# Tail of the attention in a fused decoder kernel: the last slots' work in an order written out step by step

## The reference, cut to what matters

```
x1     = x + softmax(q k^T * 1.5 / sqrt(128)) v Wout + bout       # per head, summed over 8 heads
z      = layernorm(x1);  logits = z @ router_w                    # 2048 x 8
expert = argmax(logits);  gate = 1 / sum(exp(logits - max))
pos    = running count of the tokens of that expert;  keep = pos < 256
expert_in[expert, pos] += z                                       # a scatter of rows
out    = x1 + gate * keep * (gelu(expert_in w1[e]) w2[e])[expert, pos]
```

## Time and profile before

| what | value |
| --- | --- |
| median of 3 runs | 1421.51 us (1419.95 to 1425.56) |
| the profiled execution, its own time | 1420.5 us |
| its span from first to last instruction | 1418.8 us |
| mean granted TensorE clock | 0.982 |
| PE busy over the span | 1330.4 us (94%) |
| DVE busy | 1121.2 us (79%) |
| ACT busy | 901.1 us (64%) |
| POOL busy | 881.1 us (62%) |
| last exponentials of the attention end | about 1249 us |
| first matmul of the first expert | 1314.32 us |

### The profile page before, as it was taken

The page is one execution under the profiler, slowest core; times in us unless marked ns, Lnnn a source line. Parts: engine busy times, 40 slices in busy tenths (PEclk is TensorE's granted clock), DMA queues, the critical chain, the costliest instruction groups (busy, mean ns, idle before and its releaser), DMA issues.

```text
span 1418.8 us, 20495 instructions
## 1 busy us (share of the span) xinstructions
PE 1330.4 (94%) x7244; PEld 1091.6 (77%) x7244; DVE 1121.2 (79%) x1711; ACT 901.1 (64%) x1325; POOL 881.1 (62%) x535
## 2 busy tenths in 40 slices
PE   3999999988999989999999999999999999994998
PEld 3777887887878767777777777787777778773997
DVE  6779988976811778989898998989898898985454
ACT  3534433224565577877777777777878777676674
POOL 1400011213431199998999989989989989874453
PEclk9999999999999999999999999999999999996899
DMA  9102003124666488887888888878878878787572
GB/s 278 20 9 67 2 18 109 47 76 136 232 178 213 151 229 216 212 208 192 213 210 193 216 192 208 219 179 215 210 197 210 210 175 211 182 201 263 183 243 80
DMA packets 171955, 241.22 MB, mean 170 GB/s; under 512 B 34020, under 2 KB 77414, under 8 KB 171857
## 3 DMA queue, kind: packets, MB, share of 16 engines
q1 hardware_dynamic: 156704, 210.21, 58.1%
q10 hardware_dynamic: 13104, 23.86, 5.0%
q0 software_dynamic: 2048, 5.90, 1.1%
HBM read 64.79 MB, written 41.32 MB: 75 GB/s over the span
## 4 chain that ended last, share of the span: by engine, by line
PE 51%; DVE 15%; ACT 5%; issue 4%; DMA 1%; POOL 0%; SPq 0%; ACTq 0%; DVEq 0%; POOLq 0%
PE xa_S L1476 20%; PE xa_O L1493 12%; DVE xa_mxp L1269 5%; PE xa_Y L1430 5%; PE xa_Y L1505 4%; PE ex_H L1928 3%; PE ex_Y L1940 3%; ACT xa_probs L1649 3%; PE xa_O L1430 3%; DVE xa_tq L1282 3%; DVE xa_mx_nb_rinv L1267 2%; DVE hall L1303 2%; DVE xa_mx_nb_rinv L1272 1%; DMA xa_moved<-xa_tq 0%; DVE xa_mx_nb_rinv L1298 0%
## 5 line engine op out<-in xcount | busy, mean ns | idle before, releaser
L1152 POOL TENSOR_TENSOR xa_pT<-xa_moved,xa_pT 128x1024 fp32r<-128x1024 f32 x246 | 586.1, 2406 | 35.6 <-ACT xa_pT L1643 32.4
L1476 PE MATMUL xa_S<-xa_kT,xa_qT 128*128 128x512 f32 x1536 | 397.6, 408 | 14.7 <-ACT xa_probs L1649 11.7
L1649 ACT ACTIVATE xa_probs<-xa_S,xa_mx_nb_rinv 128x1024 f32<-128x1024 f32 x256 | 286.0, 1118 | 174.6 <-DVE xa_mx_nb_rinv L1272 174.6
L1493 PE MATMUL xa_O<-xa_pT,xa_v 128*128 128x512 f32 x1536 | 375.8, 394 | 2.6 <-DVE xa_pT L1325 2.6
L1476 PEld LDWEIGHTS xa_S<-xa_kT,xa_qT 128*128 128x128 f32 x1536 | 286.3, 190 | 102.4 <-ACT xa_probs L1649 41.5
L1493 PEld LDWEIGHTS xa_O<-xa_pT,xa_v 128*128 128x128 f32 x1536 | 289.3, 189 | 68.0 <-DVE xa_pT L1325 2.9
L1282 DVE STREAM_TRANSPOSE xa_tq<-xa_probs 128x1024 f32<-128x1024 f32 x256 | 316.7, 1237 | 13.6 <-ACT xa_probs L1649 5.9
L1643 ACT ACTIVATE xa_pT<-xa_moved 128x1024 fp32r<-128x1024 f32 x254 | 253.8, 1049 | 4.1 <-DMA xa_moved<-xa_tq 3.9
L1267 DVE TENSOR_REDUCE xa_mx_nb_rinv<-xa_S 128x1 f32<-128x1024 f32 x128 | 155.6, 1215 | 79.8 <-PE xa_S L1476 77.5
L1269 DVE TENSOR_REDUCE xa_mxp<-xa_S 128x1 f32<-128x1024 f32 x128 | 157.5, 1230 | 17.7 <-PE xa_S L1476 17.7
L467 PE MATMUL fw_pp<-fw_hT,fw_wqk 128*128 128x512 f32 x384 | 100.7, 413 | 9.9 <-DVE fw_F L613 8.3
(11 more groups left out here) (228 smaller groups left out, 1812.6 us busy)
## 6 DMA issues: line engine op xcount, KB each, us to landing
xa_moved<-xa_tq SPq DMA_DIRECT2D x508, 256.0 KB, 4.5
heads_k<-ci_outs SPq DMA_DIRECT2D x32, 256.0 KB, 2.0
heads_v<-ci_outs SPq DMA_DIRECT2D x32, 256.0 KB, 2.3
heads_q<-ci_outs SPq DMA_DIRECT2D x32, 256.0 KB, 2.2
xa_chunk<-heads_v ACTq DMA_DIRECT2D x32, 256.0 KB, 3.7
ex_w1s<-in_L_ffn_w_dram SPq DMA_DIRECT2D x8, 1024.0 KB, 6.9
ex_w2s<-in_L_ffn_w_dram SPq DMA_DIRECT2D x8, 1024.0 KB, 10.0
xa_chunk<-heads_q ACTq DMA_DIRECT2D x31, 256.0 KB, 3.5
```

The costliest lines, as they stand in the source:

```text
L1152: pool.tensor_tensor(quadrants(pT[LO], r), unit_moved(r), quadrants(pT[HI], r).bitcast(F32), ALU.subtract).then_inc(lo_ready, 1)
L1476: last = pe.matmul(S[:, k], qT[a][:, i // GT % 2, q], kT[b][h % 2][:, k * 512:(k + 1) * 512], start=(n == 0), stop=(n == 2))
L1493: last = pe.matmul(O[:], v[a][:, j * P:(j + 1) * P], pT[b][:, r % PRING, k], start=(j == 0 and n == 0), stop=(j == JT - 1 and n == 2))
L1649: act.activation(probs[:, unit % RING], S[:, 2 * u:2 * u + 2].rearrange("p a b -> p (a b)"), ACT.Exp, bias=nb[:, s % 2:s % 2 + 1], scale=S ...
```

## The change

The loops over slots now end at SLOTS. What was issued behind slot 127 is written out call by call on PE, ACT and DVE. Group 31's weighted sum goes to the bank `mxp` in place of `xa_O`, and quad 2's logits and counts to S[3]. `place_rows` is split in two: the places, and the gate (`gate_rows`) with a semaphore of its own, for which the scatters wait as well. `table(0, ACT.Exp)` is dropped. Quad 3's exponentials are one activation over four tiles, of values that DVE has multiplied, with the sum taken on DVE, and two of quad 3's four tiles are scaled on DVE. DVE waits for all scatters to land before `expert_low`.

```diff
-        rp = [... for bank in (S[:, 2], S[:, 3], mxp[:], S[:, 2])]
+        rp = [... for bank in (S[:, 2], S[:, 3], S[:, 3], S[:, 2])]
...
-        END = SLOTS + 14
-        OUTPUTS = ...
-        SUMS = ...
-        ROUTING = ...
+        TAIL = SLOTS // GT - 3
+        def output_of(g):
+            return mxp if g == SLOTS // GT - 1 else O
...
             def scatter(q):
                 pool.wait_ge(slot_ready, q + 1)
+                pool.wait_ge(gated, q + 1)
                 if q < 2:
                     pool.wait_ge(scaled, q + 1)
                 else:
-                    pool.wait_ge(last_scaled, q - 1)
+                    pool.wait_ge(last_scaled, 4 if q == 2 else 6)
...
             def deviations_of_rows(q):
...
+                dve.wait_ge(rstd_rows, q + 1)
...
             def place_rows(q):
-                dve.wait_ge(expd, q + 1)
-                dve.reciprocal(rows[:, quad_rows(q), GATE], gate[:, quad(q)])
...
+            def gate_rows(q):
+                dve.wait_ge(expd, q + 1)
+                dve.reciprocal(rows[:, quad_rows(q), GATE], gate[:, quad(q)]).then_inc(gated, 1)
+            def scale_rows(tiles):
+                for i in tiles:
+                    dve.tensor_scalar(rows[:, place_of(i), 0:D], rows[:, place_of(i), X1:X1 + D], rs[:, i, 0:1],
+                                      rrstd[:, i:i + 1], ALU.subtract, ALU.mult)
...
             # VectorE behind the loop
+            transpose(SLOTS - 1, 1)
+            for k in range(2):
+                add_output(TAIL, k)
+                row_stats(TAIL, k)
+            low_parts(SLOTS - 5)
+            deviations_of_rows(0)
+            low_parts(SLOTS - 4)
+            deviations_of_rows(1)
+            choose(0)
+            low_parts(SLOTS - 3)
+            choose(1)
+            low_parts(SLOTS - 2)
+            add_outputs(TAIL + 1)
+            low_parts(SLOTS - 1)
+            statistics(TAIL + 1)
+            place_rows(0)
+            place_rows(1)
+            gate_rows(0)
+            gate_rows(1)
+            deviations_of_rows(2)
+            choose(2)
+            add_outputs(TAIL + 2)
+            place_rows(2)
+            gate_rows(2)
+            statistics(TAIL + 2)
+            choose(3)
+            deviations_of_rows(3)
+            dve.tensor_tensor(spent[:, quad(3)], ex[:, quad(3)], wide(rrstd[:, quad(3)]), ALU.mult).then_inc(rstd_rows, 1)
+            place_rows(3)
+            scale_rows(range(12, 14))
+            dve.wait_ge(expd, QUADS)
+            then(dve.reduce_sum(gate[:, quad(3)], spent[:, quad(3)], AX))
+            gate_rows(3)
+            dve.wait_ge(scattered, 16 * TILES)
             expert_low(0, w1p, w1s)
             expert_low(1, w2p, w2s)
...
             # TensorE
-                if q == 0 and g:
+                if q == 0 and 0 < g < SLOTS // GT - 1:
                     pe.wait_ge(oT_ready, g)
...
             def row_logits(q):
-                if q == QUADS - 1:
-                    pe.wait_ge(slot_ready, 1)
+                if q >= 2:
+                    pe.wait_ge(slot_ready, 2 if q == 2 else 1)
...
             # TensorE behind the loop
+            transposes_of(0)
+            weighted(SLOTS - 7)
+            out_project(TAIL, 1)
+            weighted(SLOTS - 6)
+            row_logits(0)
+            transposes_of(1)
+            weighted(SLOTS - 5)
+            row_logits(1)
+            output(TAIL + 1)
+            weighted(SLOTS - 4)
+            positions(0)
+            weighted(SLOTS - 3)
+            positions(1)
+            weighted(SLOTS - 2)
+            transposes_of(2)
+            weighted(SLOTS - 1)
+            row_logits(2)
+            output(TAIL + 2)
+            positions(2)
+            transposes_of(3)
+            row_logits(3)
+            positions(3)
...
             # ScalarE behind the loop
+            high_parts(SLOTS - 6)
+            copies(0)
+            high_parts(SLOTS - 5)
+            row_root(0)
+            row_root(1)
+            high_parts(SLOTS - 4)
+            copies(1)
+            copy_oT(TAIL + 1)
+            high_parts(SLOTS - 3)
+            row_exp(0)
+            high_parts(SLOTS - 2)
+            row_exp(1)
+            high_parts(SLOTS - 1)
+            copies(2)
+            row_root(2)
+            copy_oT(TAIL + 2)
+            scale_rows(2)
+            row_exp(2)
+            copies(3)
+            row_root(3)
+            row_exp(3)
+            scale_rows(3)
```

More of the change, by code:

```diff
@@ L847, in cross_block @@
         PJ = len(pj)
-        rp = [bank[:, 0:4 * E].rearrange("p (t e) -> p t e", e=E) for bank in (S[:, 2], S[:, 3], mxp[:], S[:, 2])]
+        rp = [bank[:, 0:4 * E].rearrange("p (t e) -> p t e", e=E) for bank in (S[:, 2], S[:, 3], S[:, 3], S[:, 2])]
         x_in = [sem(f"ci_x_in{s}") for s in range(HALVES)]
@@ L929, in among @@
             return range(EARLY + sum(AMONG[:s]), EARLY + sum(AMONG[:s + 1]))
-        END = SLOTS + 14
-        OUTPUTS = {(30, 0): 3, (30, 1): 3, (31, 0): 7, (31, 1): 7}
-        SUMS = {(30, 0): 3, (30, 1): 4, (31, 0): 7, (31, 1): 7}
-        ROUTING = {"transposes": (0, 2, 4, 8), "copies": (0, 2, 4, 8), "logits": (1, 3, 5, 9), "choose": (2, 3, 5, 9),
-                   "positions": (3, 4, 6, 10), "place": (3, 4, 6, 11),
-                   "statistics": (None, None, 4, 8), "root": (1, 1, 4, 8), "scale": (1, 2, 4, 9), "rows": (1, 2, 5, 9),
-                   "exp": (3, 3, 5, 10)}
+        TAIL = SLOTS // GT - 3
         def place_of(i):
@@ L949, in output_slot @@
         def output_slot(g, k):
-            return SLOTS + OUTPUTS[g, k] if (g, k) in OUTPUTS else (g + 1) * GT + LAG + k
+            return (g + 1) * GT + LAG + k
         def sum_slot(g, k):
-            return SLOTS + SUMS[g, k] if (g, k) in SUMS else (g + 1) * GT + LAG + 1 + k
+            return (g + 1) * GT + LAG + 1 + k
         halves_of_groups = [(g, k) for g in range(SLOTS // GT) for k in range(2)]
-        def due(what, s):
-            return [q for q, late in enumerate(ROUTING[what]) if late is not None and SLOTS + late == s]
         def finished(eng, q, k=1):
@@ L1379, in expert_low, with low_parts, add_outputs, statistics @@
                                   ALU.subtract).then_inc(e_lo, 1)
-            for s in range(END):
-                if s < SLOTS:
-                    maxima(s)
-                if 1 <= s <= SLOTS:
+            def low_parts(p):
+                low_part(2 * p)
+                low_part(2 * p + 1)
+            def add_outputs(g):
+                add_output(g, 0)
+                add_output(g, 1)
+            def statistics(g):
+                row_stats(g, 0)
+                row_stats(g, 1)
@@ L1396, in _ @@
-                for q in due("statistics", s):
-                    for k in range(2):
-                        row_stats(SLOTS // GT - 4 + q, k)
-                for q in due("scale", s):
-                    deviations_of_rows(q)
-                for q in due("choose", s):
-                    choose(q)
-                for q in due("place", s):
-                    place_rows(q)
+                transpose(s, 0)
+            transpose(SLOTS - 1, 1)
+            for k in range(2):
+                add_output(TAIL, k)
+                row_stats(TAIL, k)
@@ L1677, in row_exp @@
             def row_exp(q):
-                act.wait_ge(shifted, q + 1)
+                act.wait_ge(oh_ready, q + 1)
                 act.wait_ge(rstd_rows, q + 1)
-                for i in range(4 * q, 4 * q + 4):
-                    last = act.activation(spent[:, i], ex[:, i], ACT.Exp, scale=rrstd[:, i:i + 1], accum_out=gate[:, i:i + 1])
+                if q == QUADS - 1:
+                    act.wait_ge(rstd_rows, QUADS + 1)
+                    last = act.activation(spent[:, quad(q)], spent[:, quad(q)], ACT.Exp)
+                else:
+                    for i in range(4 * q, 4 * q + 4):
+                        last = act.activation(spent[:, i], ex[:, i], ACT.Exp, scale=rrstd[:, i:i + 1], accum_out=gate[:, i:i + 1])
                 last.then_inc(expd, 1)
@@ L1720, in _ @@
-                for q in due("copies", s):
-                    for k in range(2):
-                        copy_zt(q, k)
-                for q in due("root", s):
-                    row_root(q)
-                for q in due("rows", s):
-                    if q >= 2:
-                        table(0, ACT.Exp)
-                        scale_rows(q)
-                for q in due("exp", s):
-                    row_exp(q)
+                for c in chunks_of(s):
+                    chunk_high(c)
```

85 lines of the change are left out of this document (36 added, 49 removed).

## The result

The changed kernel took 1428.68 us (median of 7 runs, 1427.71 to 1433.02) against 1421.85 for the kernel before (7 runs, 1419.95 to 1425.56): a ratio of 1.0052, 95% interval 1.0037 to 1.0067. That is 6.8 us slower, outside the range of the prediction. The same kernel, unaltered, took 1419.54 and 1419.80 us in two later sets of runs on other occasions, while the kernel before took 1421.2 to 1421.9 in every set. The rest of this document is about that difference of 9 us.

A forecast was written before the change was run, and what follows sets the result against it. The tail was taken as bound by the order of DVE's work, then quad 3's serial chain, not transfers. Landing 4.2 us earlier less 2.6 given back is 1.6: 1421.5 - 1.6 = 1419.9 us, range 1416.5 to 1425.0.

The forecast's parts named there:

- statistics at 1291.2, choose 3 at 1293.3: DVE's tail: statistics end at 1291.2, then the choice for quad 3 follows directly and ends at 1293.3.
- low parts 127 end: DVE's tail: the last quarter's low parts end at 1277.1, 6.4 us ahead of 1283.5 in the kernel before.
- first scatter: POOL: the first scatter may start at 1281.7, 0.8 after the gate, with 1.27 from each to the next.
- last scatter: POOL: quad 3's scatters start at 1297.9, the last at 1301.7, landing at 1304.25 against 1308.47 before.
- landing to first expert: Start of the expert block: DVE's split after the landing makes this 8.45 instead of 5.85, giving 2.6 us back.
- first expert: Expert block: the first expert's matmuls begin at 1312.7, against 1314.32 in the kernel before.
- ACT's Exp load: ACT ahead of quad 3's scatters: the late table load costs 1.28, so ACT is last and rows are ready at 1297.1.
- POOL's queue becomes the bound: Rival at POOL's scatters: at pace 1.6 each, +2.3 to 1423.8, chance 0.2; at worst pace 2.3, 1434, chance 0.03.
- The table switch drains: Rival on ACT: the Exp load holds ACT another 1.4, quad 3 ready at 1298.5, kernel 1421.3; chance 0.07.
- The wait on the scatters costs nothing: Rival at the expert block: rows' transfer bounds it, not DVE's split, so all 4.2 us stay: 1417.3; chance 0.08.
- The 6.4 us go through: Rival on DVE: work behind the last low parts lies in idle time, so the kernel takes 1415.1; chance 0.04.
- The own bank: Group 31's output on PE: removes PE's wait for group 30's copy, costed at nothing because DVE is the bound there.

The follow-up runs named there:

- fourth set: The changed kernel run again, unaltered, on a later occasion beside the kernel before: 1419.54 us, ratio 0.9987; three other variants ran in the same set.
- fifth set: The changed kernel run a third time, unaltered, in a session of its own beside the kernel before: 1419.8 us, ratio 0.9986.
- The last run: The changed kernel without DVE's wait for the scatters' landing, run a second time, where nothing stalled: 1420.49 us, ratio 0.9996.
- quad 0 early: Against the changed kernel, quad 0's places and gates put right behind choose 1, so its scatters start earlier: 1420.0 us, ratio 0.999.
- the breaks on POOL: Changed kernel with a one-column POOL memset ahead of quad 1's and quad 2's scatters: 1420.0, 1419.28 and 1420.33 us in three sets.

## Why the prediction was wrong, point by point

**The step that failed** is the one sentence "statistics at 1291.2, choose 3 at 1293.3". It took for granted that quad 3's logits are known to DVE when PE has made them, as all earlier ones are. Statistics ended at 1291.6, the logits themselves at 1293.04, and choose 3 started at 1299.9. Of the 8.7 us by which it came behind the forecast, 6.8 are the late report, 1.4 the wait for matmuls that had themselves waited for a late report of the transposes, and 0.4 the statistics. The sum had no term for a late report, and the rows of the kernel before could not have priced one: its scatters come in rows of 4, with a pause at each new quad, and its logits of quad 3 are reported on time.

The same sentence puts quad 3's transposes and logits on PE at nothing, as if they always ended ahead of DVE's statistics. That fits the fourth set's run, where they end at 1291.35 and choose 3 starts right behind the statistics, and not the fifth set's, where DVE waits 1.71 us for them. It is a smaller term, left out without a reason.

**The rest of the sum held**, and the traces of the fourth and fifth set show it undisturbed:

| Step | Forecast | Result's run | Fourth set | Fifth set |
|---|---|---|---|---|
| low parts 127 end | 1277.1 | 1278.1 | 1278.5 | 1278.5 |
| first scatter | 1281.7 | 1282.6 | 1282.9 | 1283.0 |
| choose 3 starts | 1291.2 | 1299.9 | 1291.5 | 1293.0 |
| last scatter | 1301.7 | 1310.6 | 1302.4 | 1303.7 |
| landing to first expert | 8.45 | 8.0 | 8.0 | 8.0 |
| first expert | 1312.7 | 1321.1 | 1312.9 | 1314.3 |

In the landing's row the start of DVE's first split stands for the landing. The 8.0 comes out 0.45 under the forecast: 0.45 instead of 0.6 behind DVE, and 1.2 instead of 1.33 from L1961 to the matmuls make up part of it. ACT's Exp load is the last thing ahead of quad 3's scatters, as forecast: they start 0.88 behind ACT's last scaling in both undisturbed traces. The kernel's time was forecast as 1419.9 and is 1419.5 and 1419.8 where nothing stalled; the gain over the kernel before was forecast as 1.6 and is 2.3 and 1.4. That the numbers agree so closely is in part luck, as steps up to 1.4 late (low parts) and 0.45 early (the expert block) offset one another, and one program's choose 3 differs by 1.5 from trace to trace.

**The rivals.** *POOL's queue becomes the bound* named the right neighbour and the wrong victim. With DVE's wait in place the scatters never stretched: in rows of 12 and 16 all but the first took 0.97 to 1.03. What suffered was the report of another engine's work. *The table switch drains* is refuted: L1732's load takes 1.28 and the exponential follows 0.01 us behind it, in the result's run and in the others. *The wait on the scatters costs nothing* fell in the form it had, since the expert block did start behind DVE's split (1309.91, 0.45 after it). The last run shows why dropping DVE's wait gains nothing: without it the scatters pay. For those stretched scatters the Trainium skill, SBUF — State Buffer, section "Who interferes with whom", has the rule that a VectorE instruction with two SBUF inputs contends with a GpSimd one that reads SBUF, through an exclusive lock. The two stretched scatters, 2.81 and 1.90 us beside L1383, agree, if a scatter counts as an instruction that reads SBUF, which no run here tests; the same section of the Trainium skill also tells of a probe in which a tensor_tensor did not stall a DMA, and the two here did. The scatters that had no such neighbour took 0.97 or 0.98, and so did the one that started at 1299.10, before DVE's split began at 1300.05: the instruction that started second was stretched, and DVE's splits kept their 2.29. *The 6.4 us go through* fell too: in the fourth set's run low parts 127 end 5.0 us earlier than before, and the first expert starts only 1.4 earlier.

**Parts costed at nothing.** The own bank may not be free: with the old banks choose 3 starts 2.0 us sooner and the kernel is 1.1 us faster in its median, though the intervals overlap, and choose 3 varies by 1.5 between traces of one program. What the traces tie to the banks is PE's wait for places 1, 0.77 us; the rest of the 2.0 can't be told from the slower clock of one trace. Loading Exp's table late costs about 0.6 by the medians, again within what the intervals allow. The order of places and gates (quad 0 early) is worth nothing where there is no stall, 1420.0 against 1419.5 and 1419.8, and 8.5 us where there is one.

**What stays open** is the cause of the stall. Shown is that, on the occasions on which it occurs, it goes with the length of POOL's row, and that it also needs something that isn't in the program or the chip. One reading is that recording does it. The Trainium skill, NOTIFIC — the notification-queue block, section "7.1 Overflow: three behaviours, one of which stalls the engine", says that the unit which writes the records holds back its producers when its inner queues are full, rather than lose a record there. That would account for a late report and not for the missing ones, and every run here, the timed ones too, was recorded. No run here shows it. A run without recording wasn't tried, nor was a stalled set with the breaks on POOL in it.

## What to carry to other kernels

Measure a changed kernel on more than one occasion before you explain a difference below one per cent: repeated rounds of one occasion agreed within 5.3 us of each other and were 9 us from the next. Read an idle gap whose releaser is "remote" against the end of the work it waited for; if that work was done in time, look at what else was being reported. Spreading scatters out cost nothing that these runs can tell: the order with quad 0 early took 1420.0 where the other took 1428.5, and the other took 1419.5 and 1419.8 where nothing stalled.

## What the hardware showed that was not expected

A semaphore of PE rose 6.8 us after its matmul ended, while POOL issued 12 scatters 1.28 us apart, and 1.2 us after it beside 8 of them; the changed kernel had 0.01 us on two other occasions, beside rows of 16 and 12. In the stalled sets the lateness stayed at 6.8 when the twelve scatters moved no rows. POOL's scatters issued at a steady 0.97 plus 0.30 us for as long as 16 of them. In every trace here the scatters that took longer (1.18 to 2.81, apart from the 1.22 of the very first) had started while one of DVE's large two-input instructions was running; those that had started ahead of such an instruction kept their 0.97 or 1.22.
